# A graph network kernel whose TensorE signals twice a block instead of seven or twelve times

## What is computed

```
def layer0(x, src, dst, edge_attr):          # GRU on summed messages
    h = relu(concat(x[src], edge_attr) @ W1.T + b1)
    agg = segment_sum(h @ W2.T + b2, dst)
    gi, gh = agg @ Wih.T + bih, x @ Whh.T + bhh
    r, z = sigmoid(i_r + h_r), sigmoid(i_z + h_z)
    n = tanh(i_n + r * h_n)
    return (1 - z) * n + z * x
def layer1(x):                               # mean over col, at row
    agg, deg = segment_sum(x[dst], src), segment_sum(1, src)
    return (agg / max(deg, 1)) @ weight + x @ root_weight + bias
x = layernorm(x + layer0(x, ...)); out = layernorm(x + layer1(x))
```

## Time and profile before

| | |
|---|---|
| median of three runs | 5913.37 us (5907.3 to 5916.59) |
| the profiled execution's own time | 5894.56 us |
| its span, first to last instruction | 5892.9 us |
| granted TensorE clock, mean | 0.837 of 2.4 GHz |
| busy: TensorE matmul, weight load | 4424.1 us (75%), 3765.1 us (64%) |
| busy: VectorE, ScalarE, GpSimd | 3327.6 us (56%), 2357.5 us (40%), 3209.3 us (54%) |
| DMA | 998.71 MB, mean 169 GB/s |

### The profile page before, as it was taken

The page is one execution under the profiler, slowest core; times in us unless marked ns, Lnnn a source line. Parts: engine busy times, 40 slices in busy tenths (PEclk is TensorE's granted clock), DMA queues, the critical chain, the costliest instruction groups (busy, mean ns, idle before and its releaser), DMA issues.

```text
span 5892.9 us, 89839 instructions
## 1 busy us (share of the span) xinstructions
PE 4424.1 (75%) x30332; PEld 3765.1 (64%) x30332; DVE 3327.6 (56%) x9964; ACT 2357.5 (40%) x4278; POOL 3209.3 (54%) x3198
## 2 busy tenths in 40 slices
PE   6577777777777777777777777777777777777776
PEld 5465666666666666666666666667666666666664
DVE  4444656565656555555656565656565656555555
ACT  2244343434343434344444434343434343434343
POOL 2566555655565555555555656555655555555510
PEclk8667989798978888888888888879797989888889
DMA  6444747575656566565656575647575656566556
GB/s 192 91 127 137 197 141 207 150 200 149 190 162 184 168 174 174 166 184 158 187 156 194 151 201 151 197 141 206 149 202 150 194 158 186 163 179 171 169 146 176
DMA packets 1017762, 998.71 MB, mean 169 GB/s; under 512 B 204167, under 2 KB 857548, under 8 KB 1016921
## 3 DMA queue, kind: packets, MB, share of 16 engines
q1 hardware_dynamic: 830878, 459.88, 28.2%
q10 hardware_dynamic: 84075, 321.56, 17.1%
q0 software_dynamic: 102352, 211.43, 14.6%
HBM read 655.22 MB, written 337.22 MB: 168 GB/s over the span
## 4 chain that ended last, share of the span: by engine, by line
PE 50%; another core or an unknown queue 16%; DVE 15%; issue 10%; ACT 6%; DMA 1%; DVEq 1%; POOL 0%; SPq 0%; ACTq 0%; POOLq 0%
PE stream_pse L1199 12%; PE stream_psa L1208 10%; PE stream_psw L1223 9%; PE stream_pse L1191 6%; PE stream_psw_third L1223 5%; DVE stream_col L969 4%; ACT stream_a_sb L884 4%; DVE stream_sums L979 3%; DVE stream_sums L983 2%; ACT stream_hid L846 1%; DVE ring L947 1%; PE stream_psw L1247 1%; DVE stream_acc L939 1%; DVE stream_row L964 1%
## 5 line engine op out<-in xcount | busy, mean ns | idle before, releaser
L829 POOL DMA_INDIRECT ring<-y,ring x3105 | 3137.7, 1011 | 2314.9 <-ACT stream_hid L846 1492.4
L884 ACT CAST stream_a_sb<-stream_psa 98x512 f16<-98x512 f32 x3125 | 1768.8, 585 | 2909.1 <-PE stream_psa L1208 1125.5
L947 DVE TENSOR_TENSOR ring<-stream_pse,ring 128x384 f32<-128x384 f32 x1250 | 612.2, 490 | 1862.9 <-remote 836.8
L1208 PE MATMUL stream_psa<-stream_col,stream_row 128*98 128x256 f16 x6250 | 1291.4, 311 | 477.6 <-ACT stream_a_sb L884 289.0
L1223 PE MATMUL stream_psw<-stream_z,stream_strip 128*128 128x257 f16 x5850 | 936.4, 293 | 382.4 <-DVE stream_sums L983 333.1
L1208 PEld LDWEIGHTS stream_psa<-stream_col,stream_row 128*98 128x98 f16 x6250 | 823.9, 143 | 623.6 <-issue 392.2
L1199 PE MATMUL stream_pse<-w1b,ring 128*128 128x128 f32 x6250 | 1154.8, 325 | 49.8 <-issue 23.8
L1199 PEld LDWEIGHTS stream_pse<-w1b,ring 128*128 128x128 f32 x6250 | 997.7, 231 | 101.2 <-issue 61.1
L969 DVE TENSOR_TENSOR stream_col<-iota_lo,stream_twin 128x1536 f16<-128x1536 f16 x1250 | 1022.2, 818 | 0.0
L1223 PEld LDWEIGHTS stream_psw<-stream_z,stream_strip 128*128 128x128 f16 x5850 | 594.0, 105 | 542.1 <-issue 306.2
L1191 PEld LDWEIGHTS stream_pse<-stream_seg,stream_hid 128*128 128x128 f32 x6250 | 836.2, 211 | 1.1
(11 more groups left out here) (203 smaller groups left out, 2063.8 us busy)
## 6 DMA issues: line engine op xcount, KB each, us to landing
A<-stream_a_sb ACTq DMA_DIRECT2D x625, 490.0 KB
stream_strip<-A SPq DMA_DIRECT2D x1862, 160.0 KB
ring<-in_ea_blocks_dram SPq DMA_DIRECT2D x625, 160.0 KB
ring<-y,ring POOLq DMA_INDIRECT x3125
stream_col<-A SPq DMA_DIRECT2D x84, 96.0 KB, 2.5
prologue_xt<-in_xT_dram SPq DMA_DIRECT2D x14, 448.0 KB
y<-prologue_ysb SPq DMA_DIRECT2D x14, 448.0 KB
ring<-r SPq DMA_DIRECT2D x49, 128.0 KB, 2.5
```

The source lines that it names most:

```text
L829: nc.gpsimd.indirect_dma_start(out=yg[s.c % 4][:, t, :], out_offset=None, in_=h.y, in_offset=bass.IndirectOffsetOnAxis(ap=idx[s.c // (PH / ...
L884: nc.scalar.copy(a_sb[s.c % AR][0:RW, j, :], psa[BANK[j]][0:RW, :]).then_inc(a_out, 1)
L947: V.tensor_tensor(yg[s.c % 4][:, lo:hi, :], pse[half][:, 0:(hi - lo) * D].rearrange("p (t d) -> p t d", d=D), yg[s.c % 4][:, lo:hi, :], AL ...
L1208: last = nc.tensor.matmul(psa[BANK[j]][0:RW, e * LOS:(e + 1) * LOS], row1[s.c % 2][:, 2 * j + e, :], col1[s.c % 2][:, 2 * j + e, :], start ...
```

## The change

TensorE's matmuls and their order stay. Their signals become one semaphore, `step_done`, raised twice a block: by the last matmul of `counts(s, 2)`, and by a drain at the end of the block's products and units, ahead of the gate work. `e_done`, `a_done` and the streaming part's `unit_done` go; `unit_done` stays for the last stage. All readers wait for one of the two steps.

```
+FRONT = 3
 ...
             # TensorE
             def edge_product(s, half):
                 ...
-                last.then_inc(e_done, 1)
             def counts(s, j):
                 ...
-                reach(pe, a_out, s.times(PAIRS, SPENT[j]))
+                reach(pe, a_out, s.times(PAIRS, j - 2))
-                    last = nc.tensor.matmul(psa[BANK[j]][0:RW, ...
-                last.then_inc(a_done, 1)
+                    last = nc.tensor.matmul(psa[s.times(PAIRS, j) % 3][0:RW, ...
+                return last
             def unit(ph, u):
                 ...
-                last.then_inc(unit_done, 1)
+                return last
             def body(s, k=None, ph=None):
                 ...
-                counts(s, 2)
+                last = counts(s, 2)
+                last.then_inc(step_done, 1)
                 ...
                 counts(s, 4)
                 next_unit()
+                pe.drain().then_inc(step_done, 1)
                 if k is not None:
                     gate_work(k, ph)
             # ScalarE
-                    act.wait_ge(a_done, s.times(PAIRS, j + 1))
-                    nc.scalar.copy(a_sb[s.c % AR][0:RW, j, :], psa[BANK[j]][0:RW, :]).then_inc(a_out, 1)
+                    act.wait_ge(step_done, s.times(2, 1 if j < FRONT else 2))
+                    nc.scalar.copy(a_sb[s.c % AR][0:RW, j, :], psa[s.times(PAIRS, j) % 3][0:RW, :]).then_inc(a_out, 1)
             # VectorE
             def add_gathered(s, half):
-                dve.wait_ge(e_done, s.times(2, half + 1))
+                dve.wait_ge(step_done, s.times(2, half + 1))
-            def unit_first(ph, u):
-                dve.wait_ge(unit_done, ph.n(TS, u + 2))
+            def unit_first(s, ph, n, u):
+                dve.wait_ge(step_done, s.times(2, 1 if n < 2 else 2))
             def body(s, k=None, ph=None):
+                work = list(enumerate(units))
+                front = [(unit_first, w) for w in work[:2]] + [(unit_second, w) for w in work[:2]]
+                back = []
+                for w in work[2:]:
+                    back.append((unit_first, w))
+                    if w[0] > 2:
+                        back.append((unit_second, work[w[0] - 1]))
+                if work[2:]:
+                    back.append((unit_second, work[-1]))
                 ...
                 segment_hot(s)
-                adds(1)
+                adds(front, 1)
                 if more:
                     rows(nxt)
-                adds(2)
+                adds(front, 2)
                 if more:
                     cols(nxt, 0)
+                adds(front, 1)
                 add_gathered(s, 1)
                 if s.c >= 1:
                     add_segment(s.back(1), seg_at[x])
-                adds(3)
+                adds(back, 3)
                 if more:
                     cols(nxt, 1)
-                adds(99)
+                adds(back, 99)
             # SP
-                reach(sp, e_done, s.times(2, -2))
+                reach(sp, step_done, s.times(2, -2))
                 ...
-                            sp.wait_ge(unit_done, ph.n(TS, 2 * (c - RING) + 3))
+                            sp.wait_ge(unit_added, ph.n(TS, 2 * (c - RING) + 3))
```

More of the change, by code:

```diff
@@ L701, in stream @@
         idx_in, ea_in, a_stored = h.idx_in, h.ea_in, m.sems("a_stored", AR)
-        e_done, sum_done, relu_done = m.sem("e_done"), m.sem("sum_done"), m.sem("relu_done")
+        step_done, sum_done, relu_done = m.sem("step_done"), m.sem("sum_done"), m.sem("relu_done")
         seg1_ready, agg_done = m.sem("seg1_ready"), m.sem("agg_done")
-        twin_ready, hot_ready, a_done, a_out = m.sem("twin_ready"), m.sem("hot_ready"), m.sem("a_done"), m.sem("a_out")
+        twin_ready, hot_ready, a_out = m.sem("twin_ready"), m.sem("hot_ready"), m.sem("a_out")
         ea_ready, cleared, rolled = m.sem("ea_ready"), m.sem("cleared"), m.sem("rolled")
@@ L763, in body @@
                 if k == 10 and ph.p == ITER:
-                    sp.wait_ge(unit_done, ITER * TS + 1)
+                    sp.wait_ge(unit_added, ITER * TS + 1)
                     for c in range(RING - 1):
@@ L807, in _ @@
                     if c >= 1:
-                        sp.wait_ge(unit_done, ITER * TS + 1 + 2 * c)
+                        sp.wait_ge(unit_done, 2 * c)
                     load_strip(LAST[0], c + RING - 1, strip[(c - 1) % RING], strip_in[(c - 1) % RING])
@@ L869, in gate_work @@
                     if not ph.col:
-                        act.wait_ge(unit_done, ph.n(TS, 1))
+                        act.wait_ge(unit_added, ph.n(TS, 1))
                     nc.scalar.activation(zz[:, 0:T, 0:D], xb[:, 0:T], ACT.Copy, scale=SCALE).then_inc(hi_ready, 1)
@@ L936, in add_segment @@
             def add_segment(s, at):
-                dve.wait_ge(e_done, s.times(2, 4 if s.c < BLOCKS - 1 else 3))
+                dve.wait_ge(step_done, s.times(2, 4 if s.c < BLOCKS - 1 else 3))
                 reach(dve, agg_done, s.times(1))
@@ L962, in rows @@
                 dve.wait_ge(twin_ready, s.times(1, 1))
-                reach(dve, a_done, s.times(PAIRS, -PAIRS))
+                reach(dve, step_done, s.times(2, -2))
                 V.tensor_tensor(row1[s.c % 2][:].rearrange("p g (a b) -> p g a b", b=2), paired(RW, GB),
@@ L972, in segment_hot, with unit_second @@
             def segment_hot(s):
[L973 removed]
+                reach(dve, step_done, s.times(2))
                 V.tensor_tensor(seg1[s.c % 2][:], wide(h.seg_key[:, bass.ds(s.times(BT), BT)], SEGW),
                                 tall(h.iota_lo[:, 0:SEGW], BT), ALU.is_equal).then_inc(seg1_ready, 1)
[L977 to L978 removed]
+            def unit_first(s, ph, n, u):
+                dve.wait_ge(step_done, s.times(2, 1 if n < 2 else 2))
                 V.tensor_tensor(sums[:, u, :], sums[:, u, :], psw[(u + 2) % 3][:, 0:P + 1], ALU.add).then_inc(unit_part, 1)
[L981 removed]
+            def unit_second(s, ph, n, u):
                 dve.wait_ge(unit_part, ph.n(TS, u + 1))
@@ L1052, in body, with adds @@
                 units = units_of(k) if k is not None and ph.p < ITER else []
-                ops = [(f, u) for u in units for f in (unit_first, unit_second)]
-                order = []
-                for n, u in enumerate(units):
-                    order.append((unit_first, u))
-                    if n:
-                        order.append((unit_second, units[n - 1]))
-                if units:
-                    order.append((unit_second, units[-1]))
-                def adds(n):
+                work = list(enumerate(units))
[7 more added lines that the diff above has]
+                    back.append((unit_second, work[-1]))
+                def adds(order, n):
                     for _ in range(n):
                         if order:
-                            f, u = order.pop(0)
-                            f(ph, u)
+                            f, (turn, u) = order.pop(0)
+                            f(s, ph, turn, u)
                 if k == 0:
@@ L1119, in add_high @@
             def add_high(c):
-                dve.wait_ge(unit_done, ITER * TS + 2 * c + 3)
+                dve.wait_ge(unit_done, 2 * c + 2)
                 V.tensor_tensor(sums[:, 2 * c:2 * c + 2, :], sums[:, 2 * c:2 * c + 2, :], pair[c % 2][:, :, 0:P + 1], ALU.add
@@ L1205, in counts @@
                     pe.wait_ge(hot_ready, s.times(2, 1 if j == 0 else 2))
-                reach(pe, a_out, s.times(PAIRS, SPENT[j]))
+                reach(pe, a_out, s.times(PAIRS, j - 2))
                 for e in range(2):
-                    last = nc.tensor.matmul(psa[BANK[j]][0:RW, e * LOS:(e + 1) * LOS], row1[s.c % 2][:, 2 * j + e, :],
+                    last = nc.tensor.matmul(psa[s.times(PAIRS, j) % 3][0:RW, e * LOS:(e + 1) * LOS], row1[s.c % 2][:, 2 * j + e, :],
                                             col1[s.c % 2][:, 2 * j + e, :], start=True, stop=True)
-                last.then_inc(a_done, 1)
+                return last
             def unit(ph, u):
@@ L1267, in next_unit @@
                     if units:
-                        unit(ph, units.pop(0))
+                        return unit(ph, units.pop(0))
                 pe.wait_ge(ea_in[s.c % 2], s.turn(2, 16))
@@ L1301, in _ @@
             node_part(0)
-            segment(Step(0, BLOCKS - 1)).then_inc(e_done, 1)
+            segment(Step(0, BLOCKS - 1)).then_inc(step_done, 1)
             pe.wait_ge(xq_ready, LAST[1].n(1, 1))
```

5 lines of the change are left out of this document (1 added, 4 removed).

## The result

The changed kernel took 6022.39 us (median of four runs, 6016.98 to 6033.29), the kernel before 5914.98 on the same chip (5907.3 to 5921.28). The ratio is 1.0185 (95% interval 1.0165 to 1.0204): slower, and clear of noise, where the prediction had 5615 us. The profiled execution of the change has a span of 6017.2 us at a mean TensorE clock of 0.845.

What follows compares the result with a forecast made beforehand. Bound taken: a cycle of held TensorE signals and GpSimd's gathers, 8.85 us a block, no engine. 5894.6 us less 200 (blocks with units) and 95 (blocks without) gave 5600; with 18.8 for the runs' median, 5615 us, range 5380 to 6080.

Steps and rivals of the forecast that it cites:

- What bounds the kernel: Blocks with units: TensorE's signals held back during GpSimd's gathers close a cycle of 8.85 us; no engine is the bound.
- Fewer signals: TensorE raises 2 signals a block instead of 12 with units or 7 without; costed at 0.
- The drain: End of each block on TensorE: its signal not held, 0.1 us allowed for emptying; if held, 1.5 to 3.3 us.
- I take the first: Choice between two bounds for the drain's signal: not held (0.03 us, 0.1 allowed) over held (1.5 to 3.3 us).
- the loop: Held TensorE signal to next run of gathers 1.60 us, run 6.4, run's end to next held signal 0.85: 8.85 us.
- the second rival: Drain held too, its signal 0.85 us after the gathers' end, so the 8.85 us cycle stays: 5870 to 5930 us; chance 0.18.
- The schedule with units, 3.2 and 4.0 us: Block with units: 3.2 us from second `step_done` signal to first, 4.0 from first to second; period 7.2 us before any hold.
- The hold of step 1, 0.9 us: Lateness of the first `step_done` signal, 1.6 us into a run of gathers: 0.9 us, ends 0.2 and 1.9.
- the first rival: First `step_done` signal held long, 1.9 us, giving blocks with units a period of 9.3 us: 6080 us; chance 0.27.
- Blocks without units, 95 us gained: Second held signal goes, VectorE's 4.66 us wait for the first stays: 5 us a phase over 19 phases, ends 0 and 265.
- What would show it: Second gathered add within 0.2 us of the drain, blocks with units about 8.3 us, unattributed waiting well below 16%, clock over 0.84.
- The sign named for being wrong: VectorE's second gathered add still coming 0.8 us after a run of gathers ends, which would mean the drain is held.

Runs made afterwards that it cites:

- without the hold: Sets in which TensorE's signals came on time during GpSimd's gathers; the kernel before took 4579 to 4588 us there.
- With the hold: Sets in which TensorE's signals came late during GpSimd's gathers; the kernel before took 5880 to 5927 us there.
- gated gathers: Kernel before with two more waits on GpSimd, ahead of a block's first and fourth gather, for TensorE's signals: 1.0093, 1.0085, 1.0072, all without the hold.

## Why the prediction was wrong

*What bounds the kernel.* Right for the first measurement: one gather a block took most of the hold away, and 26% of the time. What I didn't see is that it needn't be there. The same kernel without the hold takes 4585 us, and there TensorE bounds the blocks with units (96% busy, with a drain added).

*Fewer signals, 0.* Nothing contradicts it: four signals a block in place of twelve or seven came out at 1.0016. By the Trainium skill (TensorE: Matmul & The Clock Gate, The cost: per-tile semaphore tail), 26.3 ns each for 8 x 360 + 3 x 265 signals fewer would be an estimate of up to 97 us. Within the 0.3% of this comparison, whose kernel also differs in its waits, none of it shows.

*The drain.* **The step that failed is "I take the first": that a drain is not held.** It is held, 1.41 us behind the last matmul in blocks with units, and VectorE's add behind it comes 0.85 us after the run of gathers, as behind the signal that it replaced. With this one choice the loop is closed again, as the second rival had it: add to next run 1.52 us (before 1.82), the run 6.65 (before 6.22), run's end to next second add 0.85 (before 0.91), 9.02 us in place of 8.95, as means over neighbouring blocks with units. The argument against that rival was that an engine with nothing left to do would report itself idle. The rows say no: an engine whose last report is held isn't idle for a drain. The Trainium skill's sentence (PSUM — Partial Sum Buffer, Engine vs sequencer instructions), that a drain waits until the engine is fully idle, agrees with the trace if idle means reported complete.

*The schedule with units, 3.2 and 4.0 us.* Right to 0.05 us, as the runs without the hold show: 3.16 and 4.04. With the hold the pace was 9.02 us.

*The hold of step 1, 0.9 us.* In blocks with units it was 0.02 us, below my lower end; in the others about 0.5. So the first rival, which put 6080 us on it, gives nearly the measured time by the wrong mechanism.

*Blocks without units, 95 us gained.* Wrong in sign. I took the second hold to go and the first to stay. In fact either step can be held, and the waits are later: GpSimd used to get ahead, the second gathered add coming 0.32 us before the end of the run of gathers in the mean over neighbouring blocks without units; in the change it comes 0.49 us after it. Their period rose from 8.40 to 8.70 us. Counted from one second gathered add to the next, all blocks without units take 61 us more, about half of the loss of 124. Another 43 us come at the first block with units of each phase (10.5 us before, 12.9 in the change), for which the prediction had no term of its own, and 21 in the other blocks with units. The second rival's price, 5870 to 5930 us, left the first two out, which is why it falls 100 us short though its mechanism was right for the blocks with units.

*The readers' waits.* They had no term of their own. I counted the new order of a block with units, but not that an add which waits for a later matmul is the start of the relu, the next gathers and the next block's products. Alone they cost 2.1% with the hold and, in the change, 5.0% without it. What they cost in the change with the hold, beside the drain, stays open.

*What would show it.* The unattributed share fell to 1%, as said, and that meant nothing; the clock rose to 0.845; both happened in a slower kernel. The sign named for being wrong, the second gathered add 0.8 us after the run's end, is what the profile shows.

*The gathers.* I had them constant. They lasted 3271.9 us in all, before 3137.7. Of 3,105 gathers 949 took over 1.0 us, before 602; the row at 2708.91 (1.69 us beside 0.94 for an undisturbed one) runs with VectorE's column comparison from 2708.84. Of the 903 gathers in the change in whose first 0.9 us VectorE ran nothing, none took over 1.0 us; the 609 with the comparison of 1536 elements there took 1.41 us in the mean. The Trainium skill (SBUF — State Buffer, SBUF: two separate sides) says that a VectorE instruction with two inputs in SBUF and a GpSimd instruction that reads SBUF exclude each other at the port pair that they share. The overlap fits that; no run moved the comparison by itself.

**Still open:** what a drain costs by itself where signals are held; how the loss divides between it and the late waits there; why the first block with units of a phase takes 2.4 us more; whether gated gathers help; why a signal at one place of a run passes in 14 ns and at others waits; and what makes one set have the hold and another not. One rival stands untested: that the recording of the trace plays a part. With the hold fewer signals have a record, 1026 of the change's 1251 steps against 1249 without it, and no run here is known to be without a recording.

## What to carry to other kernels

Before a signal is merged with a later one, list who waits for it and what that work starts: a wait moved to a later matmul cost 2 to 5% here, and the signals saved were worth nothing that could be measured. A drain was no way around late completion reports: it came as late as they did, and stopped its engine too. And where a time rests on a stall that no engine explains, run the unchanged kernel elsewhere before pricing the cure: here the stall of 22% was absent in five of the seven later sets.

## What the runs showed of the hardware that was not expected

- The same kernel took 5880 to 5927 us in some sets and 4579 to 4588 in others, with equal gathers (0.94 us for an undisturbed one). With the longer time 29% of TensorE's signals have a record within 25 ns of the matmul, 96 to 99% in the kernel with a drain at 4627 us.
- The hold needs GpSimd's gathers: with a fifth of them, 4363 us in a set where the full kernel took 5880.
- A drain on TensorE waits with the held signals: 1.41 us behind the last matmul in blocks with units (0.02 without the hold), up to 7.0 in the others.
- Not every signal during a run is held: the change's first step, 1.4 to 3.0 us into it, came within 0.06 us in 359 of 360 blocks with units.
